# A four-layer network on one core: the hand-over from the Mamba layer to the expert layer is reordered, and each token tile gets a place of its own

## The chip, the cores and the metric

The kernel runs on one core of one Trainium2 chip. The metric is the device time of one execution in microseconds, and the lower the better. Three timed runs of the kernel before gave 2579.55, 2576.08 and 2584.2 us, so the median is 2579.55 us.

## What is computed

The input is x, 4 sequences of 512 tokens with 512 channels. Four sublayers are added to it one after the other, and the input of each sublayer is a gate: a two-sided decayed scan over the tokens of exp(k) and exp(k)*v, their quotient times sigmoid(x). In shorthand of the reference:

```python
x = x + mamba2(wkv(r=x, k=v=fside, w, u, cond), ...)        # layer 0
x = x + moe_ffn(wkv(r=x, k=v=fside, w2, u2, cond), ...)     # layer 0: 8 experts, top 2 of 8
x = x + attention(wkv(r=x, ...), ...)                       # layer 1: 16 heads, causal
x = x + ffn(wkv(r=x, ...), ...)                             # layer 1

num = nf + nb - ekv + euk * v ; den = df + db - ek + euk    # forward and backward scans
out = sigmoid(r) * (num / maximum(den, 1e-8)) * (0.8 + 0.2 * tf)

logits = tok @ gate_w.T + gate_b ; top_vals, top_idx = top_k(logits, 2)
routing = softmax(top_vals)                                 # each token goes to two experts
```

The factor num/den does not depend on x. It is computed ahead of time, on other engines, beside the layers, and is kept in DRAM ("gates"). Only sigmoid(x) has to wait for x.

## The kernel before, in words

Data lies by channel: XT holds x as 4 chunks of 128 channels (KC = 4) by 2048 tokens. There are five instruction streams, and each runs in the order in which it is written; semaphores tie them together.

**Mamba layer.** A loop runs over the four sequences b. In each, TensorE (PE) projects, ScalarE (ACT) does the activations, VectorE (DVE) the convolution taps, masks and sums. Near its end PE runs the output products (L2335) into four banks, one per channel chunk m. ACT takes the square root of the mean square (L959), DVE inverts it (`rms_inv`, L1690), and for m = 0 to 3 scales a bank (L1704) and adds it to XT (L1706, semaphore `x_added`). Between these pieces the gates of later layers are worked through in pairs of 2 tiles: ACT takes exponentials (L435, L436), DVE clamps, scans (L450, L463), takes denominators (`dens`, L478) and one reciprocal for the pair (`inverse`, L485), POOL multiplies and adds (L494 to L520), and SP stores the pair and loads the next one. The last pair of this layer is `G_MOE - 1`, in slot 0 of the gate buffers (`g_v[:, 0:2]`).

**Hand-over to the expert layer.** In the last pass of the loop (b = 3) the expert layer's inputs of sequences 0 to 2, which are finished, are made: ACT takes tanh of XT (L871, into the single buffer `tx_moe`, a part of `xdt`) and DVE multiplies it with the fetched gate in `uf1` (`moe_input`, L1506). Before the change these three stand between the four scale-and-add steps of the last sequence, so that each tanh waits for the product ahead of it to free the buffer. Sequence 3 follows in four parts (L970, L1728) as its chunks of XT are added.

PE then goes through 16 token tiles of 128 tokens (NT = 16). For tile a it transposes four 128 x 128 blocks into one of three banks (L2339), runs two filler products (`keep_busy`, L348, into a spare bank), and four logit products of 8 columns (L2359). From a = 3 on it first waits until the copy of tile a - 3 has left its bank. Ahead of tile 3 there are 12 more fillers, ahead of tile 7 there are 16. ACT (L534, even tiles) and DVE (L532, odd tiles) copy each bank into `ut`, which has 4 places, so a copy of tile a + 4 waits until SP has stored tile a in DRAM (`u_tok`, L632). SP reaches these stores only after it has stored the last gate pair.

**Routing and the first block.** With all logits there, DVE computes the top two, the places of all tokens and the gather lists in some 60 small steps (L1736 to L1831). POOL then gathers blocks of 128 tokens (L763 to L765; an indirect DMA from `u_tok`). PE transposes a block (`inputs_T`), ACT and DVE split it in two parts (L994, L1857), and PE multiplies with the split weights of an expert (L2390 to L2392). The weights are split on ACT (`split_hi`, L1025) and DVE (`split_lo`, L1842) in three pieces per expert. After the first block comes a loop over the other blocks. ACT takes the exponentials of the next gate pair (`gate(moe_pair(0), ...)`) ahead of its first block's work; the second half of these waits until POOL has finished the first result of the pair before it (`P_READY[0]`).

Of the kernel before, what the change touches and what calls it, by code (L numbers as in the profile page):

```python
# [19 lines left out]
P = 128  # L20
BATCH, T, C = 4, 512, 512
KC = C // P
# [69 lines left out]
def network(nc, xT, fT, condT, cols_d, rows_d, w_in_d, w_out_d, moe_d, gw_d, bias_d, rc_d, att_d, ffn_d, outT):  # L92
# [6 lines left out]
    with ctx:  # L99
# [74 lines left out]
        tx_moe = xdt[:, 0:2, :].rearrange("p a (h t) -> p (a h) t", h=2)  # L174
        with ExitStack() as s:
# [10 lines left out]
            bias_u = sb("bias_u", [P, 3, 2 * I_MOE], F32, s)  # L186
            idx = sb("idx", [P, NBLK], I32, s)
# [3 lines left out]
        bias_dn = g_v[:, 0:2, :]  # L191
        with ExitStack() as s:
# [13 lines left out]
            with ExitStack() as s2:  # L206
                ut = sb("ut", [P, 4, C], F32, s2)
# [75 lines left out]
        ut_stored = [sem(f"ut_stored{i}") for i in range(4)]  # L283
# [45 lines left out]
        IN_PARTS = 3  # L329
        S_, TT_, PP = bank[0:3], bank[3:5], bank[5:8]  # L330
# [192 lines left out]
        def token_copies(eng, b):  # L523

            odd = eng is nc.vector
            for tb in range(1 if odd else 0, TB, 2):
                a = b * TB + tb
                eng.wait_ge(ut_T, a + 1)
                if b:
                    eng.wait_ge(ut_stored[tb], 16 * b)  # L530
                if odd:
                    nc.vector.tensor_copy(ut[:, tb, :], UT[a % 3][:]).then_inc(ut_copied[1], 1)  # L532
                else:
                    nc.scalar.activation(ut[:, tb, :], UT[a % 3][:], ACT.Copy).then_inc(ut_copied[0], 1)  # L534
# [21 lines left out]
        def _(sp):  # L556
# [13 lines left out]
            def gates(b, last):  # L570
# [62 lines left out]
            sp.wait_ge(g_out[0], FIRST_DMA + 16 * ((G_MOE + 1) // 2))  # L633
# [53 lines left out]
        def _(pool):  # L687
# [67 lines left out]
            pair_gate(G_MOE - 1, (G_MOE - 1) % 2)  # L755
# [13 lines left out]
            for i in range(4):  # L769
                pool.wait_ge(ut_stored[i], 16 * (NT // 4))  # L770
            for j in range(3):
                gather(j, j)
            with pool.Fori(0, NBLK // MOE_BLOCKS) as trip:
# [62 lines left out]
        def _(act):  # L836
# [46 lines left out]
            with act.Fori(0, BATCH) as b:  # L883
# [73 lines left out]
                square(PAIRS - 1)  # L957
                act.wait_ge(ssq_done, PAIRS * (b + 1))
# [1770 lines left out]
```

## Time and profile before

| what | us |
|---|---|
| median of three runs | 2579.55 |
| the profiled execution, device time | 2580.49 |
| span of its trace | 2578.8 |
| PE busy | 2272.5 (88%) |
| VectorE busy | 1859.4 (72%) |
| ScalarE busy | 1002.0 (39%) |
| GpSimd (POOL) busy | 676.6 (26%) |

In all rows times are microseconds from the start of the span. DVE is VectorE, ACT is ScalarE, POOL is GpSimd and SP issues DMAs. "PEclk" is the TensorE clock that was granted: 1.00 is 2.4 GHz and 0.50 is 1.2 GHz. A timeline row gives start, duration of the whole merged piece, engine, line, what it writes and reads, how many instructions it merges, and in square brackets how long the engine stood idle before it and what ended that.

### The profile page before, as it was taken

What the parts mean: (1) busy time and instruction counts of PE and PEld (TensorE: products, weight loads), DVE (VectorE), ACT (ScalarE), POOL (GpSimd) and SP (SyncE); (2) the same over time, 40 slices, a digit from 0 to 9 for tenths busy, and PEclk for the clock granted to TensorE, in tenths of its full rate; (3) what the DMA queues carried; (4) which work ended last, traced back from release to release, by engine and by line L of the source; (5) the groups of instructions that cost most, each with busy time, mean ns of one, the idle gap of its engine ahead of it and who ended that gap; (6) DMA issues with size and microseconds to landing.
All of it is one profiled execution on the core that took longest, in us unless ns stands there. A gap on an engine that the chain in (4) does not pass through costs nothing.

```text
span 2578.8 us, 34195 instructions
## 1 busy us (share of the span) xinstructions
PE 2272.5 (88%) x10449; PEld 1672.1 (65%) x10450; DVE 1859.4 (72%) x2835; ACT 1002.0 (39%) x2073; POOL 676.6 (26%) x544
## 2 busy tenths in 40 slices
PE   0789989899898889778877999999999997999998
PEld 0344444444445677666666888888887876788886
DVE  8989898888996655556645668777777775666665
ACT  2243352352442443444434344434444443322222
POOL 5434434344342433324341011212212210000000
PEclk9999999999998899989988999999999998999999
DMA  5000001010024432343151000010000201000001
GB/s 206 17 33 33 33 16 49 17 49 18 31 82 174 154 119 66 127 164 127 60 198 46 1 33 16 17 37 21 17 29 13 65 17 49 25 25 24 24 12 65
DMA packets 52807, 148.66 MB, mean 58 GB/s; under 512 B 5008, under 2 KB 5008, under 8 KB 48336
## 3 DMA queue, kind: packets, MB, share of 16 engines
q1 hardware_dynamic: 34144, 96.08, 10.5%
q10 hardware_dynamic: 12864, 32.81, 3.5%
q0 software_dynamic: 5680, 18.62, 2.4%
q14 instruction: 97, 0.79, 0.1%
q8 instruction: 22, 0.36, 0.1%
HBM read 113.14 MB, written 34.34 MB: 57 GB/s over the span
## 4 chain that ended last, share of the span: by engine, by line
PE 37%; issue 31%; POOL 11%; DVE 8%; POOLq 6%; ACT 3%; DMA 1%; ACTq 1%; DVEq 0%; SPq 0%; another core or an unknown queue 0%
PE bank L340 9%; PE bank L341 9%; PE bank L342 9%; PE bank L2339 3%; POOLq L495 2%; POOL g_v L503 2%; POOL g_v L496 2%; PE bank L2390 2%; PE bank L2391 2%; PE bank L2392 2%; POOLq L521 1%; PE bank L2454 1%; POOLq L518 1%; POOLq L507 1%; POOL g_s L517 1%
## 5 line engine op out<-in xcount | busy, mean ns | idle before, releaser
L2214 PE MATMUL bank<-um,w_in 128*128 128x512 f32 x576 | 262.4, 609 | 3.3 <-DVE lm L1562 3.1
L2214 PEld LDWEIGHTS bank<-um,w_in 128*128 128x128 f32 x576 | 109.5, 195 | 134.8 <-issue 127.8
L340 PE MATMUL bank<-u_hi,aw_hi 128*128 (+1 forms) x384 | 158.9, 414 | 13.0 <-DVE u_lo L1955 9.1
L1182 ACT ACTIVATE probs<-bank,nmx 128x128 f32<-128x128 f32 (+3 forms) x256 | 131.5, 527 | 92.7 <-DVE nmx L1978 92.7
L1189 ACT ACTIVATE pt_hi<-bank 128x512 fp32r<-128x512 f32 (+1 forms) x192 | 94.1, 526 | 166.8 <-PE bank L2339 166.0
L341 PE MATMUL bank<-u_lo,aw_hi 128*128 (+1 forms) x384 | 152.0, 396 | 0.0
L342 PE MATMUL bank<-u_hi,aw_lo 128*128 (+1 forms) x384 | 151.9, 396 | 0.0
L1993 DVE TENSOR_TENSOR pt_lo<-bank,pt_hi 128x512 fp32r<-128x512 f32 (+1 forms) x192 | 108.8, 593 | 44.1 <-ACT pt_hi L1189 40.2
L340 PE MATMUL bank<-u_hi,fw_hi 128*128 128x512 f32 x352 | 136.9, 389 | 0.0
L341 PE MATMUL bank<-u_lo,fw_hi 128*128 128x512 f32 x352 | 136.9, 389 | 0.0
L342 PE MATMUL bank<-u_hi,fw_lo 128*128 128x512 f32 x352 | 136.9, 389 | 0.0
L2390 PE MATMUL bank<-mw,bu_hi 128*128 (+1 forms) x312 | 127.4, 408 | 10.6 <-DVE mw L1842 6.1
L450 DVE TENSOR_TENSOR_SCAN g_s<-decay,g_s 128x512 f32<-128x512 f32 x96 | 128.7, 1382 | 10.5 <-POOL g_v L496 10.5
L502 POOL TENSOR_TENSOR g_eu<-g_eu,g_s 128x512 f32<-128x512 f32 x48 | 65.6, 1366 | 253.8 <-DVE g_s L463 253.8
L1975 DVE TENSOR_REDUCE rinv<-bank 128x1 f32<-128x128 f32 (+3 forms) x256 | 107.7, 483 | 32.5 <-PE bank L2496 32.3
L2339 PE MATMUL bank<-ident,probs 128*128 128x128 f32 x640 | 94.3, 279 | 40.9 <-DVE pt_lo L1993 18.6
L463 DVE TENSOR_TENSOR_SCAN g_s<-decay,g_s 128x512 f32<-128x512 f32 x96 | 112.3, 1211 | 19.4 <-issue 18.4
L2391 PE MATMUL bank<-mw,bu_hi 128*128 (+1 forms) x312 | 123.5, 396 | 0.0
L2392 PE MATMUL bank<-mw,bu_lo 128*128 (+1 forms) x312 | 123.4, 396 | 0.0
L2162 DVE SCALAR_TENSOR_TENSOR XT<-bank,cols,XT 128x512 f32<-128x512 f32 x176 | 119.9, 742 | 3.4 <-PE bank L342 3.4
L2335 PE MATMUL bank<-xa,w_out 128*128 128x512 f32 x256 | 111.8, 592 | 0.0
L1288 ACT ACTIVATE f_t<-bank,f_sc 128x512 f32<-128x512 f32 x44 | 30.2, 687 | 209.5 <-PE bank L342 208.8
(385 smaller groups left out, 6235.3 us busy)
## 6 DMA issues: line engine op xcount, KB each, us to landing
m_stage<-in_moe SPq DMA_DIRECT2D x21, 1024.0 KB, 7.1
y_slot<-m_o ACTq DMA_DIRECT2D x39, 256.0 KB, 2.6
g_v<-in_fT SPq DMA_DIRECT2D x18, 512.0 KB, 3.3
gates<-g_v SPq DMA_DIRECT2D x18, 512.0 KB, 2.8
f_stage<-in_ffn SPq DMA_DIRECT2D x11, 768.0 KB, 4.3
u_g<-gates SPq DMA_DIRECT2D x8, 1024.0 KB, 10.1
aw_in<-in_att SPq DMA_DIRECT2D x4, 1280.0 KB
w_in<-in_w_in ACTq DMA_DIRECT2D x1, 4640.0 KB, 16.8
```

The lines of the kernel that those rows point to most:

```text
L340: nc.tensor.matmul(out, hi_w, hi_x, start=start, stop=False)
L341: nc.tensor.matmul(out, hi_w, lo_x, start=False, stop=False)
L342: return nc.tensor.matmul(out, lo_w, hi_x, start=False, stop=stop)
L450: nc.vector.tensor_tensor_scan(x, d, x, 0.0, ALU.mult, ALU.add).then_inc(g_vec, 1)
L463: nc.vector.tensor_tensor_scan(x[:, ::-1], d, x[:, ::-1], 0.0, ALU.mult, ALU.add).then_inc(g_vec, 1)
L1182: A(probs[:, h % 2, PR_AT[qb]:PR_AT[qb] + w], S_[bk][:, c0:c0 + w], ACT.Exp, bias=nmx[:, h % 2, qb:qb + 1], scale=SCALE, accum_out=rsum[:, ...
L2162: V.scalar_tensor_tensor(xm, FD[m][:], col("down_s", m), xm, ALU.mult, ALU.add).then_inc(fx_acc, 1)
L2214: mm = M(dst[:], w_in[:, k, c0:c0 + P], um[:, k, :], start=(k == 0), stop=(k == KC - 1))
L2339: return nc.tensor.transpose(out, src, ident[0:dim, 0:dim])
L2390: M(out, x_hi[:, kc, :], hi, start=False, stop=False, skip_group_check=True)
L2391: M(out, x_hi[:, kc, :], lo, start=False, stop=False, skip_group_check=True)
L2392: mm = M(out, x_lo[:, kc, :], hi, start=False, stop=(kc == KC - 1), skip_group_check=True)
```

## The change

- Expert inputs of sequences 0 to 2 (tanh on ACT, product on DVE) stand ahead of the square root and the reciprocal of the last sequence's norm. Each has its own tanh buffer (`um` and two parts of `xdt`).
- The last gate pair's scans, `dens` and `inverse` leave the loop for b = 3. The scans come after the inputs of sequence 3 on DVE, `dens` ahead of the last token copy, `inverse` after the routing tables, ahead of the first weight split. On POOL its `gate_result` comes after the first three gathers. SP stores it after the weight loads of expert 1.
- `ut` has 16 places. ACT copies tiles 0 to 11 and DVE tiles 12 to 15. No copy waits for a store.
- The down bias has its own buffer. SP issues the first up bias after all token stores have landed.
- Fillers ahead of tile 3 go from 12 to 6, ahead of tile 7 from 16 to none. The two per tile are kept.
- On ACT the exponentials of `moe_pair(0)` go from ahead of the first block's work to just ahead of the loop. On DVE `u_lo_split(0)` comes ahead of the second piece of the weight split.

```diff
-        tx_moe = xdt[:, 0:2, :].rearrange("p a (h t) -> p (a h) t", h=2)
+        tx_moe = [um[:], *(xdt[:, i:i + 2, :].rearrange("p a (h t) -> p (a h) t", h=2) for i in (0, 2))]
+            bias_dn = sb("bias_dn", [P, 2, C], F32, s)
-        bias_dn = g_v[:, 0:2, :]
-                ut = sb("ut", [P, 4, C], F32, s2)
+                ut = sb("ut", [P, NT, C], F32, s2)
+        ACT_TILES = 3 * TB
+        LAST_PAIR = G_MOE - 1, (G_MOE - 1) % 2
...
+        def token_copy(eng, a):
+            eng.wait_ge(ut_T, a + 1)
+            if eng is nc.vector:
+                nc.vector.tensor_copy(ut[:, a, :], UT[a % 3][:]).then_inc(ut_copied[1], 1)
+            else:
+                nc.scalar.activation(ut[:, a, :], UT[a % 3][:], ACT.Copy).then_inc(ut_copied[0], 1)
...  SP
-                    g_store(sp, G_MOE - 1, 0)
+            for a in range(NT):
+                sp.wait_ge(*copies(a))
+                sp.dma_start(u_dram[a * P:(a + 1) * P, :], ut[:, a, :]).then_inc(ut_stored, 16)
+            sp.wait_ge(ut_stored, 16 * NT)
             up_bias(0)
-            for a in range(NT):
-                sp.wait_ge(ut_copied[a % 2], a // 2 + 1)
-                sp.dma_start(u_dram[a * P:(a + 1) * P, :], ut[:, a % 4, :]).then_inc(ut_stored[a % 4], 16)
             for e in range(1, E):
                 stage(e)
+                if e == 1:
+                    g_store(sp, *LAST_PAIR)
...  POOL
-            pair_gate(G_MOE - 1, (G_MOE - 1) % 2)
+            for t in range(2):
+                gate_products(pool, *LAST_PAIR, t)
+            for t in range(2):
+                gate_add(pool, *LAST_PAIR, t)
+            gate_den_product(pool, *LAST_PAIR)
...
             for j in range(3):
                 gather(j, j)
+            gate_result(pool, *LAST_PAIR)
...  ACT
                 square(PAIRS - 1)
+                with act.If(b == BATCH - 1):
+                    act.wait_ge(x_added, KC * (BATCH - 1))
+                    for nxt in range(BATCH - 1):
+                        tanh_x(BATCH + nxt, nxt, tx_moe[nxt], None)
                 act.wait_ge(ssq_done, PAIRS * (b + 1))
...
-            for m in range(KC - 1):
+            for m in range(KC):
                 last_sequence(m)
-            token_copies(act, 0)
-            last_sequence(KC - 1)
             for p in range(M_PIECES):
                 o = slice(p * M_PIECE, (p + 1) * M_PIECE)
                 act.dma_start(m_stage[:, o], moe_d[0][:, o]).then_inc(m_staged[p], 16)
-            for b in range(1, BATCH):
-                token_copies(act, b)
+            for a in range(ACT_TILES):
+                token_copy(act, a)
...
-            gate(moe_pair(0), 0)
-            gate(moe_pair(0), 1)
             u_hi_copy(0)
             up_tanh(0, 0)
             fill_up(packed_of(1, True), 1)
             u_hi_copy(1)
+            gate(moe_pair(0), 0)
+            gate(moe_pair(0), 1)
...  DVE
-                scans(fourth, 0)
-                scans(fourth, 1)
+                with dve.If(b < BATCH - 1):
+                    scans(fourth, 0)
+                    scans(fourth, 1)
+                with dve.If(b == BATCH - 1):
+                    for m in range(BATCH - 1):
+                        moe_input(m)
...
+            scans(LAST_PAIR, 0)
+            scans(LAST_PAIR, 1)
+            for a in range(ACT_TILES, NT):
+                if a == NT - 1:
+                    dens(LAST_PAIR)
+                token_copy(dve, a)
...
             dve.wait_ge(route_vec, TAB_READY)
+            inverse(LAST_PAIR)
...
             split_lo(0, 0, (0,))
+            u_lo_split(0)
             split_lo(0, 0, (1,))
-            u_lo_split(0)
             split_lo(0, 0, (2,))
...  PE
-                        keep_busy({3: 12, 7: 16}.get(a, 0))
-                        pe.wait_ge(ut_copied[(a - 3) % 2], (a - 3) // 2 + 1)
+                        keep_busy({3: 6}.get(a, 0))
+                        pe.wait_ge(*copies(a - 3))
```

## Rows read from the trace of the kernel before

**Rows 1.** The page's first line, the span of the profiled execution.

```profile
span 2578.8 us, 34195 instructions
```

**Rows 2.** Busy time by stretch: stretch, length, PE, PEld, DVE, ACT, POOL, PEclk, DMA share, GB/s.

```profile
764.50:768.00 3.50, 3.50 (x11) 1.18 (x9) 2.81 (x3) 2.70 (x2) 0.00 (x0) 0.52 0.00 0
...
774.80:785.00 10.20, 9.42 (x40) 8.17 (x40) 5.78 (x7) 0.63 (x1) 4.49 (x3) 0.50 0.88 324
...
788.40:805.80 17.40, 17.40 (x137) 14.98 (x136) 4.15 (x6) 3.58 (x6) 0.00 (x0) 1.00 0.56 215
```

**Rows 3.** Timeline of PE, from the last output products to token tile 15.

```profile
744.54 15.61 PE L2335 MATMUL bank<-xa,w_out 128*128 128x512 f32 x36
...
764.37 4.44 PE L348 MATMUL bank<-causal_b,ident_b 128*128 128x512 bf16 x12
...
775.58 1.09 PE L2339 MATMUL bank<-ident,uf 128*128 128x128 f32 x4 [1.58 <-DVE ut L532]
...
785.50 5.01 PE L348 MATMUL bank<-causal_b,ident_b 128*128 128x512 bf16 x16
...
792.02 0.63 PE L2339 MATMUL bank<-ident,uf 128*128 128x128 f32 x4
...
804.01 0.64 PE L2339 MATMUL bank<-ident,uf 128*128 128x128 f32 x4
```

**Rows 4.** Timeline of DVE, from the last pair's scans to the first routing step.

```profile
739.77 4.32 DVE L450 TENSOR_TENSOR_SCAN g_s<-decay,g_s 128x512 f32<-128x512 f32 x2 [1.24 <-POOL g_v L496]
...
753.47 3.33 DVE L1690 RECIPROCAL e<-e 128x512 f32<-128x512 f32 x1
...
757.41 2.29 DVE L1506 SCALAR_TENSOR_TENSOR uf<-xdt,uf 128x2048 f32<-128x2048 f32 x1
...
764.72 0.69 DVE L1706 TENSOR_TENSOR XT<-XT,lm 128x512 f32 x1
...
773.63 1.21 DVE L1706 TENSOR_TENSOR XT<-XT,lm 128x512 f32 x1
...
805.91 0.29 DVE L1736 TENSOR_TENSOR rt<-bank,rows 128x128 f32<-128x128 f32 x1 [0.53 <-PE bank L2359]
```

**Rows 5.** Timeline of ACT, its weight loads for expert 0 and its third token copy.

```profile
774.87 1.32 ACTq L979 DMA_DIRECT2D m_stage<-in_moe  x3
789.35 0.60 ACT L534 ACTIVATE ut<-bank 128x512 f32<-128x512 f32 x1 [13.85 <-DMA u_tok<-ut]
```

**Rows 6.** Timeline of SP, the token stores.

```profile
780.87 24.86 SPq L632 DMA_DIRECT2D u_tok<-ut x16
```

**Rows 7.** The tile uf: the four fetches of gates, shortest, median and longest, and their landing.

```profile
L598 SPq DMA_DIRECT2D uf<-gates x4: 405/452/670, 739.9 to 741.9; - x4
...
DMA to landing us min/median/max: 8.9/11.1/12.8
```

**Rows 8.** Timelines at the first expert block: PE.

```profile
834.58 0.50 PE L2390 MATMUL bank<-mw,bu_hi 128*128 128x512 f32 x1 [2.08 <-DVE bu_lo L1857]
...
857.11 0.66 PE L2339 MATMUL bank<-ident,m_y 128*128 128x128 f32 x4 [1.15 <-DVE bu_lo L1857]
```

**Rows 9.** Timeline of DVE, the first two pieces of the weight split.

```profile
829.43 4.49 DVE L1842 TENSOR_TENSOR mw<-m_stage,mw 128x2048 fp32r<-128x2048 f32 x2
```

**Rows 10.** Timeline of ACT, an exponential of the gate pair and the first split of expert 1.

```profile
829.05 0.61 ACT L435 ACTIVATE g_s<-g_v 128x512 f32<-128x512 f32 x1
...
846.01 1.91 ACT L1025 ACTIVATE mw<-m_stage 128x2048 f32 x1 [3.36 <-issue]
```

**Rows 11.** Timeline of POOL, a product of the last pair's result and gathers 1 to 3.

```profile
774.25 1.72 POOL L517 TENSOR_TENSOR g_s<-g_s 128x512 f32<-128x512 f32 x1
...
832.60 2.17 POOL L765 DMA_INDIRECT ug<-u_tok,idx_now  x1 [0.84 <-issue]
...
842.03 0.97 POOL L765 DMA_INDIRECT ug<-u_tok,idx_now  x1 [5.26 <-PE bank L2339]
...
846.36 0.97 POOL L765 DMA_INDIRECT ug<-u_tok,idx_now  x1 [3.16 <-issue]
```

More of the change, by code:

```diff
@@ L282, in network @@
         ut_copied = [sem(f"ut_copied{i}") for i in range(2)]
-        ut_stored = [sem(f"ut_stored{i}") for i in range(4)]
+        ut_stored = sem("ut_stored")
         route_mm, route_vec = sem("route_mm"), sem("route_vec")
@@ L521, in gate_result, with copies @@
             eng.drain()
[L523 to L534, printed above, removed]
+        def token_copy(eng, a):
[4 more added lines that the diff above has]
+                nc.scalar.activation(ut[:, a, :], UT[a % 3][:], ACT.Copy).then_inc(ut_copied[0], 1)
+        def copies(a):
+            return (ut_copied[0], a + 1) if a < ACT_TILES else (ut_copied[1], a + 1 - ACT_TILES)
         def mamba_pair(b, r):
@@ L768, in _ @@
             pool.wait_ge(route_vec, IDX_READY)
-            for i in range(4):
-                pool.wait_ge(ut_stored[i], 16 * (NT // 4))
+            pool.wait_ge(ut_stored, 16 * NT)
             for j in range(3):
                 gather(j, j)
+            gate_result(pool, *LAST_PAIR)
             with pool.Fori(0, NBLK // MOE_BLOCKS) as trip:
@@ L961, in _ @@
                     tanh_x(b + 1, (b + 1) % BATCH, txm, b + 1)
[L962 to L965 removed]
             def last_sequence(m):
                 act.wait_ge(x_added, KC * (BATCH - 1) + m + 1)
[L970 removed]
+                A(tx_moe[1][:, m, :], XT[:, m, tok(BATCH - 1)], ACT.Tanh, scale=0.5).then_inc(last_tanh, 1)
             act.wait_ge(u_ready, FIRST + 2 * BATCH - 1)
[L973 removed]
+            for m in range(KC):
                 last_sequence(m)
[L975 to L976 removed]
             for p in range(M_PIECES):
@@ L1513, in moe_input @@
             def moe_input(b):
[L1514 removed]
+                gated(BATCH + b, uf1[:, b].rearrange("p k t -> p (k t)"), tx_moe[b].rearrange("p k t -> p (k t)"), g_fetched[b], 1)
             mamba_input(0)
@@ L1692, in _ @@
                     mamba_input(b + 1)
-                dens(fourth)
+                    dens(fourth)
                 for m in range(KC):
-                    if m < BATCH - 1:
-                        with dve.If(b == BATCH - 1):
-                            moe_input(m)
-                    else:
-                        inverse(fourth)
+                    if m == KC - 1:
+                        with dve.If(b < BATCH - 1):
+                            inverse(fourth)
                     if m == 0:
@@ L1796, in _ @@
             dve.wait_ge(route_mm, U_DONE)
-            for i in range(4):
-                dve.wait_ge(ut_stored[i], 16 * (NT // 4))
+            dve.wait_ge(ut_stored, 16 * NT)
             route.inc(V.tensor_tensor(oh_r[:], choices(2, P), rconst("iota", P).unsqueeze(1).to_broadcast([P, 2 * NT, P]),
@@ L2367, in _ @@
             M(LGP[:, 256:384], ones[:], gt2, start=True, stop=True).then_inc(route_mm, 1)
-            for i in range(2):
-                pe.wait_ge(ut_copied[i], NT // 2)
+            pe.wait_ge(ut_copied[0], ACT_TILES)
+            pe.wait_ge(ut_copied[1], NT - ACT_TILES)
             pe.wait_ge(dve_step, DVE_MAMBA * BATCH + AT_PREFIX)
```

15 lines of the change are left out of this document (2 added, 13 removed).

## The prediction

> **What bounds the kernel now.** The span is 2578.8 us [rows 1]. I read the PE timeline of the stretch that the change touches first, then the other engines' timelines for what each PE gap waits for, and last the granted clock by stretch. The loop passes before the last one and everything after the first expert blocks run the same instructions in the same order, so only about 740 to 860 us can change, and what PE does there sets the start of all that follows.
>
> In this stretch PE finishes the output products at 744.54 + 15.61 = 760.15 [rows 3]. Three token tiles later it runs 12 fillers (764.37) and then loses time in three ways. The copies come late: tile 4 starts at 775.58 after an idle wait for DVE [rows 3], because DVE makes its last addition to XT only at 773.63 [rows 4]. The copies of tiles 4 to 7 then wait for a store: ACT stood idle for 13.85 us until the store of tile 0 had landed, and its copy starts at 789.35 [rows 5]; SP had issued that store at 780.87, behind the last gate pair [rows 6]. And the clock is at 0.50 from 774.8 to 785.0 [rows 2], so that tiles 4 to 6 take (785.50 - 775.58) / 3 = 3.31 us each, whereas tiles 8 to 15 take (804.01 - 792.02) / 7 = 1.71 us each at 1.00 [rows 2, 3]. From tile 8 on PE is never idle and bounds the chain. The first routing step of DVE at 805.91 [rows 4] follows the last logit product at once, and it heads a serial chain of small steps to the first weight split at 829.43 [rows 9]. So: whatever moves the end of tile 15 moves the rest one for one.
>
> **The change, part by part.**
>
> *Inputs ahead of the norm, scans away.* DVE no longer runs the pair's scans from 739.77 to 753.47 (13.7 us) [rows 4]. In their place it has three products of 2.29 us. These wait for the gates, which SP issues from 739.9 to 741.9 and which land 8.9 to 12.8 us after their issue [rows 7]: the last at about 754.7, the third, with a median of 11.1 from about 741, at about 752. So product 2 ends at 752 + 2.3 = 754.3, the reciprocal (3.33) [rows 4] at about 757.7, which is 0.9 us later than today's 753.47 + 3.33 = 756.8. The freed scans hardly help here, since the fetch is late next. The gain comes behind it: no product or tanh wait stands between the four additions. One scaling and one addition take 2 x 0.69 plus a small gap, say 1.5 us [rows 4], so the last addition ends at 757.7 + 4 x 1.5 = 763.7, against 773.63 + 1.21 = 774.84. The output products end at 760.15, in time for it. The three tanh on ACT fall into the time in which it waits for PE's sum of squares; they cost nothing unless they last beyond 752.
>
> *Token copies.* After the last addition ACT does one tanh (0.6), issues the three weight loads (1.32, which overlaps the tanh as it does at 774.87) [rows 5] and copies tile 0 (0.60): it is out at about 763.8 + 1.3 + 0.6 = 765.7, and tile 3 can start at 765.8. PE by then has its three tiles and 6 fillers behind it: 12 fillers took 4.44, partly at the low clock [rows 3], so 6 end between 765.3 and 766.5. From there no copy waits for a store, and ACT needs 0.6 us per tile against PE's 1.71, so PE runs through. Tile 15 starts at 765.8 + 12 x 1.71 = 786.4 instead of 804.01: **17.6 us earlier, if the clock is at 1.00**. The last store is issued a microsecond after that tile and has the whole routing chain (23.5 us from 805.91 to 829.43) [rows 4, 9] to land in; so has the first up bias, which now queues on SP behind the stores, and the down bias. Without this cover each would cost its landing, some 2 to 8 us.
>
> *Scans, dens, store of the last pair.* DVE has the scans (13.7) from about 766 to 780, and its first token copy is tile 12, transposed at 765.8 + 9 x 1.71 = 781.2. They fit by a hair; an overrun of 3 us would delay tile 15's bank by less than that. POOL's additions lie beside them. The store on SP goes behind expert 1's loads; the loads of expert 2 behind it wait for splits that come later anyway. I take 0 for these, between 0 and 2.
>
> *Inverse ahead of the first split.* On DVE 3.33 us are put ahead of the split at 829.43 (times from here on in the old count, so with the gain of 17.6 taken off later). One piece is 4.49 / 2 = 2.24 [rows 9]. The input's low part then follows after one piece instead of two: today it takes 834.58 - (829.43 + 4.49) = 0.66 after the second piece until PE starts, and from now on 829.43 + 3.33 + 2.24 + 0.66 = 835.7; PE's first expert product moves from 834.58 [rows 8] to 835.7, **+1.1 us**, not +3.3. Today POOL is done with the second block's gather only at 842 [rows 11], after PE's first 24 expert products, so little of it reaches the second block: I take 0.2.
>
> *Exponentials ahead of the loop.* ACT's four exponentials (0.61 each) [rows 10] lay in idle time ahead of the first block. Now they lie between the copy that ends at 846.01 - 3.36 = 842.65 and the loop's entry, which takes 3.36 us of issue before the first split at 846.01 [rows 10]. From this split hang DVE's split and its low part, on which PE waits at 857.11 [rows 8], without slack. The least cost is 4 x 0.61 + 0.2 = 2.6 us. But the second half also waits until POOL has done the third of four products of `gate_result`, which is now behind gather 2, with a drain between. Gather 1 starts at 832.60 as before. A gather that meets no weight loads takes 846.36 - 842.03 = 4.3 us, gather 1, which met them, kept POOL for 842.03 - 832.60 = 9.4 us [rows 11]. In the new order the loads start some 3 us later (the split that frees their buffer is later), so gather 1 is fast and gather 2 starts at 836.9, into the loads: POOL's drain ends at about 836.9 + 8.7 = 845.6, the third product (1.3 to 1.72) [rows 11] at 846.9. Exponentials until 848.1, loop entry 3.36: the split starts at 851.5, **+5.5 us**. If gather 1 meets the loads as well, gather 2 starts at 842.03 and ends at 851 and the cost is 10.6. So the bounds are 2.6 and 10.6, and I take 5.5, since it is built on the measured gathers. The 1.1 of the paragraph above is inside it.
>
> **The sum.** The profiled execution took 2580.49 us (span 2578.8 and 1.7 around it), 0.9 more than the median 2579.55. 2580.5 - 17.6 + 5.5 = 2568.4, and I say 2568. The clock's ups and downs in the first expert blocks shift by a few us with it; that is in the range.
>
> **The clock, the open question.** In the profile the clock fell at 764.5, with PE busy all through (3.50 of 3.50 in that stretch) [rows 2], after the three token tiles that have no fillers; it rose after the 12 fillers, and it rose again only within the 16 fillers of 785.50. From 774.8 to 785.0 PE ran token tiles with two fillers each and stayed at 0.50; from 788.4 to 805.8 it ran the same tiles and stayed at 1.00 [rows 2, 3]. So this work keeps either level that it finds, and the change takes out most of the fillers that lifted it. What decides is whether the clock falls in tiles 0 to 2, which end at 764. The new order starts these 0.3 us earlier and puts fillers right behind them as before; the trace holds one execution, in which it fell, and nothing in it says that it must fall in each. I give it 3 in 10.
> The Trainium skill, in "TensorE: Matmul & The Clock Gate", section "What's actually happening", says that the slow level is the default and that activity releases it, and its section on oscillation lays the fall to idle gaps of PE. By this rule tiles without idle time would neither lose the clock nor stay slow, and the result would be the forecast alone; the rows above show a fall and a long stay without idle time, so here the trace decides against it, and the low case stands.
>
> **The rivals.**
>
> *A. The clock falls in tiles 0 to 2 and nothing lifts it (slower).* Then tiles 3 to 15 take 3.31 us each. Tile 15 starts at 766 + 12 x 3.31 = 805.7, 1.7 later than today, and takes 1.6 longer itself: +3.3. With the 5.5 of the hand-over: 2580.5 + 3.3 + 5.5 = 2589.3. It decides from the point at which more than about 7 of the 13 tiles run at 0.50 (7 x 1.6 = 11.2 of the net 12.1 us eaten). For it: the fall at 764.5 and the 10 us at 0.50 [rows 2]. Against it: the same tiles held 1.00 for 17 us [rows 2].
>
> *B. The hand-over stalls more.* ACT's exponentials wait behind POOL's gathers at the upper bound: 2580.5 - 17.6 + 10.6 = 2573.5, and with a fall of the clock in the longer PE gap up to 2576. For it: gather 1's 9.4 us [rows 11]. Against it: the later loads.
>
> *C. The hand-over costs only the exponentials.* 2580.5 - 17.6 + 2.6 = 2565.5, a little less if some are hidden. For it: gathers of 4.3 us.
>
> *D. The change does not do what it says,* since the fetched gates (to 754.7) hold the norm up. At 3 us later for each addition this would give 2571; it is part of the range.
>
> **How the numbers follow.** Forecast with its variants (D) 0.55, at 2568 (own range 2564 to 2573); A 0.25 (0.3 of the executions, and the median needs most of them), B 0.12, C 0.08. For a range with 8 in 10 I must take in most of A: low 2562, high 2590. About 0.3% is what a measurement of this kernel can tell from no change, that is below 2571.8 or above 2587.3. Faster: 0.47 of the forecast, C, and 0.02 of B: 0.57. Same: 0.08 of the forecast, 0.10 of B, 0.07 of A: 0.25. Slower: 0.18 of A.
>
> **What would show it.** Right: the last addition to XT at about 763 to 764; no wait of a copy for a store; tile 3 to tile 15 in 20.6 us with PEclk 1.00; first routing step at about 788.3; ACT's exponentials of the pair behind its second input copy, with an idle time in the middle ended by POOL, and a PE gap of 3 to 6 us ahead of the third block's input. Wrong: PEclk 0.50 over the tiles (A); additions that still wait; a first routing step later than 792 at full clock; or no POOL wait in ACT (C). The forecast fails altogether if a stretch outside 740 to 860 moves.

## The result, and the profile after

The changed kernel took 2561.56 us (median; 2557.01 to 2565.08), beside 2579.55 (2576.08 to 2586.71) for the kernel before in the same comparison. The ratio is 0.9926, with a 95% interval of 0.9914 to 0.9937: faster by 0.74%, or 18 us. The forecast was 2568 with a range from 2562 to 2590, so the sign was right and the median lies 0.4 us below the range. Its profiled execution was the longest, 2565.08 us (span 2563.4). Of all executions of this study two lie far outside, 7877.76 us of r4_inverse_exps_early and 3646.75 us of the kernel before in the second comparison; they are left out of the medians and ratios below.

Granted clock and busy time by stretch of the kernel after (columns as in rows 2):

```profile
760.00:764.50 4.50, 4.50 (x40) 4.10 (x39) 4.07 (x7) 3.07 (x4) 0.00 (x0) 1.00 0.01 4
764.50:768.00 3.50, 1.94 (x13) 1.09 (x11) 3.50 (x6) 2.33 (x5) 0.00 (x0) 1.00 0.52 162
768.00:789.20 21.20, 21.20 (x177) 19.34 (x176) 14.32 (x16) 5.15 (x9) 7.88 (x5) 1.00 0.84 321
```

Timeline of PE, token tiles 0 to 15 and the first expert blocks, of the kernel after:

```profile
760.12 0.60 PE L2347 MATMUL bank<-ident,uf 128*128 128x128 f32 x4
...
763.93 1.46 PE L350 MATMUL bank<-causal_b,ident_b 128*128 128x512 bf16 x6
766.95 0.66 PE L2347 MATMUL bank<-ident,uf 128*128 128x128 f32 x4 [1.56 <-ACT ut L531]
...
787.53 0.64 PE L2347 MATMUL bank<-ident,uf 128*128 128x128 f32 x4
...
819.16 0.72 PE L2398 MATMUL bank<-mw,bu_hi 128*128 128x512 f32 x1 [3.15 <-DVE bu_lo L1865]
...
845.04 0.66 PE L2347 MATMUL bank<-ident,m_y 128*128 128x128 f32 x4 [0.62 <-DVE bu_lo L1865]
857.58 1.11 PE L2347 MATMUL bank<-ident,ug 128*128 128x128 f32 x4 [5.60 <-DVE by_lo L1887]
```

Timeline of DVE: the expert inputs, the norm, the last addition, the first routing step.

```profile
747.18 2.29 DVE L1510 SCALAR_TENSOR_TENSOR uf<-um,uf 128x2048 f32<-128x2048 f32 x1 [8.51 <-DMA uf<-gates]
...
753.30 2.29 DVE L1510 SCALAR_TENSOR_TENSOR uf<-xdt,uf 128x2048 f32<-128x2048 f32 x1 [0.80 <-DMA uf<-gates]
755.51 3.35 DVE L1698 RECIPROCAL e<-e 128x512 f32<-128x512 f32 x1
...
764.19 0.69 DVE L1712 TENSOR_TENSOR XT<-XT,lm 128x512 f32 x1
...
789.50 0.29 DVE L1744 TENSOR_TENSOR rt<-bank,rows 128x128 f32<-128x128 f32 x1 [0.60 <-PE bank L2367]
```

Timeline of ACT: the first token copies, the third exponential of the pair, the first split of expert 1.

```profile
766.30 2.06 ACT L531 ACTIVATE ut<-bank 128x512 f32<-128x512 f32 x4 [0.76 <-issue]
...
829.54 0.63 ACT L437 ACTIVATE g_s<-g_v 128x512 f32<-128x512 f32 x1 [0.82 <-POOL g_v L521]
...
834.15 1.92 ACT L1029 ACTIVATE mw<-m_stage 128x2048 f32 x1 [3.37 <-issue]
```

Timeline of POOL: the third product of the last pair's result, two gathers and a product of the next gate pair behind them.

```profile
828.17 1.27 POOL L521 TENSOR_TENSOR g_v<-g_v,g_s 128x512 f32<-128x512 f32 x1 [2.26 <-issue]
...
832.35 1.01 POOL L771 DMA_INDIRECT ug<-u_tok,idx_now  x1 [0.76 <-issue]
836.95 2.58 POOL L771 DMA_INDIRECT ug<-u_tok,idx_now  x1 [3.39 <-issue]
...
845.56 2.78 POOL L498 TENSOR_TENSOR g_v<-g_eu,g_v 128x512 f32<-128x512 f32 x1 [4.72 <-issue]
```

The three losses of [rows 2, 3] are gone. PE waits once more, 1.56 us ahead of tile 3, and then runs twelve tiles in 787.53 - 766.95 = 20.58 us, 1.715 each, with the clock at 1.00. No copy waits for a store. The first routing step comes at 789.50 instead of 805.91 [rows 4], 16.4 us earlier. At the first product of expert 0 the gain is 834.58 - 819.16 = 15.4 [rows 8], at the third block's input 857.11 - 845.04 = 12.1 [rows 8]. (These two rows transpose `m_y`, the second block's middle result, right ahead of the third block's first products; the prediction calls the place the third block's input, and so does the text below. `ug` at 857.58 is the input of the fourth block.) The span is shorter by 15.4.

### The profile page after: what moved, and what is told of

It reads as the page before. It is cut to its first block, busy times and chain, and to the rows that moved or that the text cites. A ratio compares the mean times of both kernels' runs of the same rounds, so it can differ in the third digit from the quotient of the medians.

```text
span 2563.4 us, 34103 instructions
## 1 busy us (share of the span) xinstructions
PE 2258.9 (88%) x10411; PEld 1666.8 (65%) x10428; DVE 1853.6 (72%) x2831; ACT 1003.0 (39%) x2076; POOL 675.8 (26%) x544
## 4 chain that ended last, share of the span: by engine, by line
PE 38%; issue 30%; POOL 10%; DVE 8%; POOLq 6%; ACT 4%; DMA 2%; ACTq 1%; another core or an unknown queue 0%; DVEq 0%; SPq 0%
PE bank L342 9%; PE bank L344 9%; PE bank L343 9%; PE bank L2347 3%; PE bank L2398 2%; PE bank L2400 2%; PE bank L2399 2%; POOLq L497 2%; POOL g_v L498 2%; POOL g_v L505 2%; POOLq L523 1%; POOLq L520 1%; POOL g_s L519 1%; POOLq L509 1%; POOL g_eu L504 1%
## 6 DMA issues: line engine op xcount, KB each, us to landing
u_g<-gates SPq DMA_DIRECT2D x8, 1024.0 KB, 10.7
```

## The experiments

All kernels compute all of the reference; only filler products, whose results nobody reads, are added or left out. Three theories stood against each other. T1, the forecast's: the tile stretch gives the gain, the hand-over to the expert blocks costs some 4 to 5 us of it, and this passes on to the end. T2: what is late in the expert blocks is another thing, so the hand-over's delay is taken back there. T3: the granted clock in the tile stretch decides, and the fillers that were kept decide the clock. "Before" is the kernel before in the same comparison, since the three comparisons ran on three chips and its median differs from one to the next (2578.14 in the first, 2572.07 in the second, 2579.85 in the third). The second one holds no execution of the changed kernel, so its runs are set against before or each other. The ratio with its interval is an estimate from all the executions and not the quotient of the two medians.

| run | median, us (lowest to highest) | before | ratio, 95% |
|---|---|---|---|
| r1_after_again | 2558.34 (2554.83 to 2577.55) | 2578.14 | 0.9939 (0.9919 to 0.9959) |
| r2_scans_back | 2570.28 (2567.18 to 2577.5) | 2578.14 | 0.9974 (0.9962 to 0.9985) |
| r3_inverse_early | 2560.44 (2559.17 to 2585.93) | 2578.14 | 0.9939 (0.9924 to 0.9954) |
| r4_inverse_exps_early | 2563.16 (2550.64 to 2569.05) | 2578.14 | 0.9947 (0.9927 to 0.9966) |
| r5_places_only | 2566.28 (2564.81 to 2575.37) | 2572.07 | 0.9981 (0.9971 to 0.9991) |
| r6_places_few_fillers | 2575.97 (2571.65 to 2584.36) | 2572.07 | 1.0018 (1.0008 to 1.0029) |
| r7_no_six | 2575.38 (2571.7 to 2578.52) | 2572.07 | 1.0014 (1.0005 to 1.0023) |
| r8_fillers_back | 2558.95 (2554.97 to 2562.55) | 2572.07 | 0.9947 (0.9933 to 0.9961) |
| r9_after_third | 2563.04 (2557.78 to 2584.4) | 2579.85 | 0.9945 (0.9926 to 0.9964) |
| r10_products_first | 2555.57 (2551.74 to 2572.47) | 2579.85 | 0.9917 (0.9895 to 0.9938) |
| r11_fill_first_three | 2567.1 (2560.89 to 2569.42) | 2579.85 | 0.9946 (0.9933 to 0.9959) |
| r12_all_three | 2554.26 (2551.69 to 2556.71) | 2579.85 | 0.9900 (0.9886 to 0.9914) |

### The changed kernel again

> The changed kernel once more, unchanged, on another chip, to see how far single executions lie apart and whether the tile stretch ever runs at the low clock. Theory 1 (the route start is set by the last addition and 13 tiles at 1.71 us; the rest of the spread comes from clock falls in the expert blocks): 2557 to 2566 us, tiles 3 to 15 in 20.6 us at PEclk 1.00, and no execution near 2580. Rival 1 (the clock falls in tiles 0 to 2 in some executions): one or two executions of five lie 18 to 22 us above the others, at 2578 to 2585.

> The changed kernel a third time, unchanged, as the yardstick for the three kernels of this call, since the kernel before gave 2578.1 us as the median of one call and 2572.1 of the other. Theory 1: 2554 to 2566 us, and, as the highest of nine executions in the first call (2577.55) hints, perhaps one execution some 18 us above the others with the tiles at the low clock.

No edit in either. The medians are 19.8 and 16.8 us below those of before; with the 18.0 of the first comparison the gain is 17 to 20 us. Of the 26 executions of this kernel three stand apart, 2577.55, 2582.99 and 2584.4, with a mean granted clock of 0.951 to 0.952 over the whole execution where the others had 0.958 or more. None of the three was traced. Rival A had them at 3 in 10. Two other kernels with the same PE tile code have one such execution each: r3 2585.93 (0.951) and r10 2572.47 (0.954). The expectation for r1 under T1 had none near 2580 and missed; its rival had one or two in five.

### What the six fillers are for

```diff
 r7_no_six, against the changed kernel
-                        keep_busy({3: 6}.get(a, 0))
 r8_fillers_back, against the changed kernel
-                        keep_busy({3: 6}.get(a, 0))
+                        keep_busy({3: 12, 7: 16}.get(a, 0))
```

> The changed kernel without the 6 fillers ahead of tile 3. PE then waits idle for about 3 us (763.9 to 766.9) for ACT's first copy. If the clock falls there and tile work does not lift it: tiles of 3.31 us, the first routing step about 18 to 20 us later, 2580 us. If the fillers there do nothing: the same time as the changed kernel within 1 us.

> The changed kernel with 12 fillers ahead of tile 3 and 16 ahead of tile 7, as before the change. At the full clock a filler is 0.21 to 0.23 us. Ahead of tile 3 the first 12 fit nearly into the wait for ACT (763.9 to 766.95); the 16 add 3.5 us to PE. Theory 1 (PE bounds the tiles and has no idle time): 3.5 us more than the changed kernel. Rival (PE has slack there): 0 to 1 us.

Busy time and granted clock by stretch of r7_no_six (columns as in rows 2):

```profile
764.50:768.00 3.50, 0.58 (x3) 0.58 (x4) 3.36 (x7) 1.94 (x5) 0.00 (x0) 0.63 0.41 122
768.00:785.00 17.00, 17.00 (x74) 14.80 (x73) 11.22 (x10) 3.33 (x6) 6.72 (x4) 0.50 0.78 300
785.00:806.00 21.00, 21.00 (x90) 18.07 (x89) 2.44 (x5) 2.39 (x4) 0.00 (x0) 0.50 0.20 76
```

Its PE timeline, tiles 3 and 15:

```profile
767.42 1.11 PE L2347 MATMUL bank<-ident,uf 128*128 128x128 f32 x4 [3.08 <-ACT ut L531]
...
807.12 1.09 PE L2347 MATMUL bank<-ident,uf 128*128 128x128 f32 x4
```

Without the six, PE stands idle for 3.08 us ahead of tile 3, the clock falls there, and all twelve tiles take (807.12 - 767.42) / 12 = 3.31 us, though PE is busy all through: 19.1 us lost up to tile 15. All executions of r7 lie between 2571.7 and 2578.5, 16 us above r8 in the median and 3 us above before; the expectation had 2580. So six bf16 products of 1.46 us in all carry nearly the whole gain of the change, seen through before's median. With all the old fillers back (r8) the clock stays at 1.00 too and tile 15 starts at 792.11, 24.0 us after tile 3 instead of 20.6: the fillers cost 3.4 us there, once nothing stalls behind them. r8 lies 13.1 us below before, where the changed kernel lies 17 to 20 below it in the other two comparisons; that fits the 3.5 us expected, without a direct comparison.

The profiled execution of r3 (its edit is below) happened to be one of the rare long ones, 2585.93 us against 2559 to 2564 for the others of its kernel, and shows what happened in it. Busy time and granted clock by stretch of r3_inverse_early:

```profile
764.50:768.00 3.50, 2.29 (x16) 1.32 (x14) 3.36 (x6) 1.56 (x4) 0.00 (x0) 1.00 0.16 29
768.00:785.00 17.00, 16.44 (x75) 14.42 (x76) 13.23 (x14) 4.37 (x9) 8.05 (x5) 0.56 0.85 319
```

Its PE timeline, tiles 3, 4 and 15:

```profile
768.56 0.66 PE L2348 MATMUL bank<-ident,uf 128*128 128x128 f32 x4 [1.77 <-ACT ut L531]
...
770.64 1.09 PE L2348 MATMUL bank<-ident,uf 128*128 128x128 f32 x4
...
807.01 1.09 PE L2348 MATMUL bank<-ident,uf 128*128 128x128 f32 x4
```

The six fillers are there, the wait ahead of tile 3 is 1.77 us instead of 1.56, and the clock falls in tile 3; from 770.64 each tile takes 3.31 us. What follows the fall is rival A's mechanism, at its price: the two long executions of r9 lie 20.0 and 21.4 us above their median, the one of r1 19.2, and the forecast had 2589.3 - 2568.4 = 20.9. That these three fell in the same way is likely by their mean clock and their time, and not traced. The Trainium skill, in "TensorE: Matmul & The Clock Gate", section "HAM oscillation — how this bites in real kernels", lays a fall to idle gaps of PE. The falls in r7 and r3 follow one. For the fall at 764.5 in the kernel before [rows 2] the prediction says that PE had no idle time, but it had, ahead of tile 0. Timeline of PE of the kernel before, tiles 0 and 7:

```profile
760.53 0.63 PE L2339 MATMUL bank<-ident,uf 128*128 128x128 f32 x4 [0.38 <-DVE lm L1704]
...
790.35 0.60 PE L2339 MATMUL bank<-ident,uf 128*128 128x128 f32 x4
```

r5 and r6, which keep the old order, have the same wait (0.38 and 0.39 us) and the same fall behind tiles 0 to 2, with PE busy in between; in the ten traces that have no wait there, the clock holds over tiles 0 to 2. So the prediction's sentence that the trace decides against that rule is not safe. Whether so short a wait is the cause was not tested by itself.

### The places alone, and with few fillers

```diff
 both, against the kernel before
-                ut = sb("ut", [P, 4, C], F32, s2)
+                ut = sb("ut", [P, NT, C], F32, s2)
...
-                if b:
-                    eng.wait_ge(ut_stored[tb], 16 * b)
 r6_places_few_fillers besides
-                        keep_busy({3: 12, 7: 16}.get(a, 0))
+                        keep_busy({3: 6}.get(a, 0))
```

> The kernel before with one part of the change alone: ut has 16 places and no copy waits for a store (the first up bias is fetched after the stores, since its buffer lies under the larger ut). Fillers stay at 12 and 16. Theory 1 (the 16 fillers ahead of tile 7 had run in the time of the store wait, so PE itself was not idle): PE's work is the same, 0 to 1 us of change against before; the ACT wait of 13.85 us for the store vanishes without effect. Rival 4 (the store wait set the pace): 5 to 9 us less than before.

> As the kernel before with 16 places, and with 6 fillers ahead of tile 3 and none ahead of tile 7, as in the change, but with the late additions of before, so that PE waits for copies at tiles 3 and 4. Rival 1's mechanism (tile work with two fillers keeps a low clock once it is low): PEclk 0.50 from about 771 to the end of tile 15, tiles of 3.31 us, the last routing input at about 775.6 + 12 x 3.31 = 815, 9 to 11 us later than before: about 2590. Theory that the clock recovers by itself within the tile work: it rises some tiles later, and the 5.0 us of fillers are saved: 2572 to 2577.

In both, SP issues the first up bias behind the token stores. ACT's copy of tile 4, which stood for 13.85 us behind a store [rows 5], no longer does. Timeline of ACT of r5_places_only, its copies of tiles 4 and 6:

```profile
777.80 0.60 ACT L532 ACTIVATE ut<-bank 128x512 f32<-128x512 f32 x1 [1.21 <-PE bank L2339]
784.41 0.60 ACT L532 ACTIVATE ut<-bank 128x512 f32<-128x512 f32 x1 [6.02 <-PE bank L2339]
```

Its PE timeline, tile 3, the sixteen fillers and tile 15:

```profile
771.98 0.76 PE L2339 MATMUL bank<-ident,uf 128*128 128x128 f32 x4 [2.07 <-ACT ut L532]
...
786.59 5.02 PE L348 MATMUL bank<-causal_b,ident_b 128*128 128x512 bf16 x16
...
805.11 0.64 PE L2339 MATMUL bank<-ident,uf 128*128 128x128 f32 x4
```

Yet tile 3 to tile 15 takes 33.1 us as before (805.11 - 771.98; 804.01 - 770.88 there): PE had spent the store wait in its sixteen fillers, so in these two traces the largest idle time of the profile was worth nothing in the tile stretch. The medians say otherwise: 2572.07 and 2566.28 are 5.8 us apart, where T1 expected 0 to 1 and the rival, that the store wait set the pace, 5 to 9. The traced execution (2571.36) lies 5.1 us above r5's median, so it can't speak for the others. In the kernel before the copy of tile 4 ended at 789.35 + 0.60 = 789.95 and PE went on at 790.35, so the fillers covered the store wait by 0.4 us only, at the clock of that execution. In the two traces r5 is 1.1 us behind at the first routing step (807.00) and 5.7 ahead at the last expert block (1270.17 and 1275.83). What the 5.8 us are stays open.

In r6 the clock falls behind tiles 0 to 2 as in the kernel before [rows 2], six fillers with a wait of 3.89 us behind them don't lift it, tiles 3 to 15 run at 0.50, and tile 15 starts at 811.61 (expected 815). The median is 9.7 us above r5's but 3.9 above before, where 9 to 11 above before were expected: the time lies in the range of the other theory (2572 to 2577), whose mechanism, a clock that rises by itself within the tiles, the trace rules out. The few fillers pay only together with the new order.

### The last pair's scans back ahead of the inputs

```diff
-                with dve.If(b < BATCH - 1):
-                    scans(fourth, 0)
-                    scans(fourth, 1)
+                scans(fourth, 0)
+                scans(fourth, 1)
...
-            scans(LAST_PAIR, 0)
-            scans(LAST_PAIR, 1)
```

> The changed kernel with the last pair's scans back in the loop, on DVE ahead of the three expert inputs, so that these start at 753.5 as the scans did end before. Theory 1: the last addition to XT ends at 753.5 + 6.9 + 3.35 + 6.0 = 769.8 instead of 764.9, so the time is 4.9 us above that of the changed kernel. Rival 2 (moving the scans brings nothing, since the fetched gates land late and the chain waits for something else): 0 to 1 us.

Timeline of DVE of r2_scans_back:

```profile
741.11 4.34 DVE L452 TENSOR_TENSOR_SCAN g_s<-decay,g_s 128x512 f32<-128x512 f32 x2 [1.26 <-POOL g_v L498]
...
754.83 2.27 DVE L1510 SCALAR_TENSOR_TENSOR uf<-um,uf 128x2048 f32<-128x2048 f32 x1
757.01 6.62 DVE L1510 SCALAR_TENSOR_TENSOR uf<-xdt,uf 128x2048 f32<-128x2048 f32 x2
763.56 3.34 DVE L1697 RECIPROCAL e<-e 128x512 f32<-128x512 f32 x1
```

Its POOL timeline at the same time:

```profile
754.99 3.23 POOL L504 TENSOR_TENSOR g_eu<-g_eu,g_s 128x512 f32<-128x512 f32 x1 [2.48 <-DVE g_s L465]
758.18 3.31 POOL L505 TENSOR_TENSOR g_v<-g_v,g_s 128x512 f32<-128x512 f32 x1
```

The reciprocal comes at 763.56 instead of 755.51, 8.05 us later. I had expected 4.9. The scans began 1.3 us later than in the kernel before, and two of the products took 3.35 us each instead of 2.29; together 3.4, about what was missing. POOL's additions lie beside them, but the first product lies beside one as well and took 2.27, so what made the two long is not shown. Tile 0 then starts at 767.9 instead of 760.12, the tiles run at 0.50 until the clock rises at 779.4 in tile 3, behind the six fillers and with no wait between, and the median is 12 us above r1's. So moving the scans was needed: the sentence "the freed scans hardly help here" is right only against the old order, in which no product stood ahead of the norm. With the products ahead, the scans' move is worth 12 of the 20 us.

### The hand-over, undone in two steps

```diff
 r3_inverse_early, against the changed kernel
-                if a == NT - 1:
+                if a == ACT_TILES:
                     dens(LAST_PAIR)
                 token_copy(dve, a)
+                if a == ACT_TILES:
+                    inverse(LAST_PAIR)
...
-            inverse(LAST_PAIR)
...  POOL
+            gate_result(pool, *LAST_PAIR)
             for j in range(3):
                 gather(j, j)
-            gate_result(pool, *LAST_PAIR)
 r4_inverse_exps_early besides, on ACT
+            gate(moe_pair(0), 0)
+            gate(moe_pair(0), 1)
             u_hi_copy(0)
...
             u_hi_copy(1)
-            gate(moe_pair(0), 0)
-            gate(moe_pair(0), 1)
```

> The changed kernel with the last pair's dens ahead of DVE's first token copy, its inverse right behind that copy, where DVE waits for PE, and gate_result on POOL ahead of the gathers. The exponentials stay ahead of the loop. Theory 1 (the inverse in front of the first split and POOL behind the gathers cost the hand-over): the first expert product starts 1.6 us earlier against the last routing step, PE's gap there falls from 3.15 to about 1.5 us, which also spares the low clock behind it, and the first split of expert 1 starts 3.8 us earlier: 3 to 4 us less time. Rival 3 (the expert blocks take up a late start, since PE waits there anyway): 0 to 1 us.

> As the kernel with the early inverse, and ACT's exponentials of the next pair back ahead of the first block's work, where ACT is idle. Theory 1: another 2.5 us (four exponentials of 0.61) in front of the split of expert 1, so 5.5 to 6.5 us less than the changed kernel: about 2555. Rival 3: no difference to the kernel with the early inverse beyond 1 us.

Neither gains, where 3 to 4 and 5.5 to 6.5 us were expected: 2560.44 and 2563.16, beside 2558.34 for r1. Timeline of PE of r4_inverse_exps_early, at the third block and behind it:

```profile
839.46 0.66 PE L2348 MATMUL bank<-ident,m_y 128*128 128x128 f32 x4 [0.42 <-DVE bu_lo L1866]
856.65 1.11 PE L2348 MATMUL bank<-ident,ug 128*128 128x128 f32 x4 [10.20 <-DVE by_lo L1888]
```

Its DVE timeline, the next pair's scans:

```profile
847.64 4.28 DVE L452 TENSOR_TENSOR_SCAN g_s<-decay,g_s 128x512 f32<-128x512 f32 x2 [5.91 <-POOL g_v L498]
```

Its POOL timeline, a gather and the product that the scans wait for:

```profile
831.95 0.97 POOL L772 DMA_INDIRECT ug<-u_tok,idx_now  x1 [7.40 <-issue]
...
846.22 1.26 POOL L498 TENSOR_TENSOR g_v<-g_eu,g_v 128x512 f32<-128x512 f32 x1 [6.65 <-issue]
```

The two steps do what T1 says up to the third block: its input is transposed at 839.46 instead of 845.04, 5.6 us earlier (0.5 of it is there at the first routing step already, 788.96 and 789.50). Then PE stands for 10.20 us instead of 5.60, and the next block's `ug` comes at 856.65 instead of 857.58: 4.7 of the 5.6 are given back. What is late there is POOL's product (L498) of the next gate pair. It stands on POOL behind two gathers and a drain (an instruction of the kernel between L496 and L498), comes at 846.22 against 845.56 in the changed kernel, however early ACT was, and DVE stands idle ahead of its scans until then, with the `by_lo` that PE waits for behind them. This is T2, up to this block.

### POOL's products ahead of the gathers

```diff
+                gate_products(pool, k, s, 0)
+                gate_products(pool, k, s, 1)
                 ahead(0)
                 ahead(1)
-                gate_products(pool, k, s, 0)
-                gate_products(pool, k, s, 1)
                 ahead(2)
```

> The changed kernel with one swap on POOL: in each pass of the expert loop the two gate products stand ahead of the two gathers. Theory 2 (what is late after the hand-over is POOL: the product on which DVE's forward scan waits is queued behind gathers 3 and 4, which are slow beside the weight loads, and DVE's low part of the block, on which PE waits 5.6 us, is queued behind that scan): the PE gap ahead of the fourth block's input falls from 5.6 to about 3 us, 2 to 3 us less time. Rival 5 (the gap is set by the scans themselves): no change within 1 us.

If the product's place behind the gathers is what is late, this must gain where r3 and r4 didn't. Timeline of POOL of r10_products_first, its last product of the pair:

```profile
835.92 1.29 POOL L498 TENSOR_TENSOR g_v<-g_eu,g_v 128x512 f32<-128x512 f32 x1
```

Its PE timeline, at the third block, behind it and at the last block:

```profile
844.89 0.60 PE L2347 MATMUL bank<-ident,m_y 128*128 128x128 f32 x4
853.34 0.86 PE L2347 MATMUL bank<-ident,ug 128*128 128x128 f32 x4 [2.22 <-DVE by_lo L1887]
...
1250.54 0.60 PE L2347 MATMUL bank<-ident,m_y 128*128 128x128 f32 x4
```

The products end at 837.2, PE's wait falls from 5.60 to 2.22 us, and its `ug` comes 4.2 us earlier with the same start at the third block. The median is 2555.57, 7.5 us below the changed kernel's 2563.04 in the same comparison, though the two intervals overlap by 0.1%. That is more than the 2 to 3 us expected: the swap acts in every pass of the expert loop, and the last expert block comes at 1250.54, against 1255.46 to 1260.85 in the three traces of the changed kernel. T2 is confirmed for this wait.

### Fillers in tiles 0 to 2, and all together

```diff
 r11_fill_first_three, against the changed kernel (r12_all_three has r4's and r10's edits as well)
-                    if a >= 3:
-                        keep_busy(2)
+                    keep_busy(2)
```

> The changed kernel with two fillers in tiles 0 to 2 as well. These lie in the time in which PE waits for ACT's first copy anyway (idle 1.56 us). Rival 1's mechanism (the clock falls, in some executions, over the tiles without fillers, and stays low to the end of tile 15): the same median within 2 us, but no execution 15 to 25 us above the others. If the slow executions come from elsewhere, they stay.

> The early inverse, the early exponentials, the gate products ahead of the gathers and the fillers in tiles 0 to 2 together. Theory 2: the early hand-over gained 5.6 us up to the second block and lost 4.7 of it in a PE gap of 10.2 us, in which DVE waited for POOL's product. With the products first the gap is 3 to 5 us and the gain stays: 5 to 8 us less than the changed kernel, about 2551 to 2555. Rival 3 (the expert blocks take up a late start by themselves): no gain beyond that of the kernel with the products first.

PE timeline of r12_all_three, at the same places:

```profile
840.76 0.66 PE L2348 MATMUL bank<-ident,m_y 128*128 128x128 f32 x4 [1.19 <-DVE bu_lo L1866]
849.89 0.65 PE L2348 MATMUL bank<-ident,ug 128*128 128x128 f32 x4 [0.69 <-DVE by_lo L1888]
...
1249.14 0.60 PE L2348 MATMUL bank<-ident,m_y 128*128 128x128 f32 x4
```

r11 starts tile 15 at 786.9, like the changed kernel, and shows no execution at the low clock, but with 3 in 26 for the changed kernel five executions can't show that it prevents them; its median is 4 us higher. In r12 PE waits 0.69 us ahead of `ug`, which comes 7.7 us earlier than in the changed kernel, so the early hand-over gets past the wait that took it back in r4. But it does not last to the end. Set against r10, which has POOL's products first and the late hand-over, r12 is 4.1 us ahead at the third block (844.89 - 840.76), and 1.4 at the last (1250.54 - 1249.14), about what it had at the first routing step (788.52 against 789.82). The medians are 1.3 us apart, with intervals that overlap, so the rival of r12's expectation, no gain beyond r10's, is not refuted: the expert blocks took the early start back a second time, and by what is open. At 2554.26 us, ratio 0.9900, it is the fastest kernel of the study, 25.6 us below before and 8.8 below the changed kernel.

## Why the prediction was right or wrong

**Inputs ahead of the norm: right, within 1.3 us.** The last product ended at 753.30 + 2.29 = 755.6 (forecast 754.3), each held up by its fetch as said (SP issued the fetches from 740.93 instead of 739.90), and the last addition at 764.19 + 0.69 = 764.9 (763.7, from 774.84).

**Copies and tiles: right.** Tile 3 at 766.95 (765.8), then 20.58 us to tile 15 (20.6). The first routing step came 16.4 us earlier instead of 17.6, which is the 1.2 us of the late fetch. Scans, `dens`, stores and the bias loads cost nothing that shows. D, additions that wait for the fetch by 3 us each time, did not come.

**Hand-over up to the third block: right to 0.3 us in place, 1.2 us too dear.** The first expert product lost 16.4 - 15.4 = 1.0 us (1.1). The third of POOL's products ended at 829.44 (846.9 - 17.6 = 829.3), the exponentials followed it, and the first split came at 834.15 (851.5 - 17.6 = 833.9). At the third block the gain was 12.1, as the sum had it; but from a first routing step that was 16.4 earlier, not 17.6, so the hand-over cost 4.3 us up to there instead of 5.5, and the two errors cancel. B and C fall: gathers 1 and 2 did not both meet the loads, and there was a wait for POOL.

**From there to the end: the step that failed.** "Whatever moves the end of tile 15 moves the rest one for one", and with it the 5.5 us of the hand-over, put into the sum whole. r4 shows that undoing it brings 5.6 us at the third block, 0.9 one block later and 1.1 at the last expert block; r12 against r10 shows 4.1 at the third block and 1.4 at the last. So a late or early hand-over is for the most part taken up within the expert blocks, at first by the wait for POOL's product; what takes up the rest is open. With 16.4 and some 1 us instead of 17.6 and 5.5, the sum is 2580.5 - 16.4 + 1 = 2565.1, and the profiled execution took 2565.08. That fit is better than its proof, and partly luck: in the pair of profiles themselves the gain is 12.1 at the third block, falls to 10.7 and grows to 15.0 only by the last one. What made it grow is not shown. Timeline of PE of the kernel before, the last expert block:

```profile
1275.83 0.60 PE L2339 MATMUL bank<-ident,m_y 128*128 128x128 f32 x4
```

The same of the kernel after:

```profile
1260.85 0.60 PE L2347 MATMUL bank<-ident,m_y 128*128 128x128 f32 x4
```

Besides, between the third block and a later one the profiled executions of the changed kernel differ among themselves by up to 4.6 us.

**The width: the range lacked a term.** It was built from mechanisms, for one execution, and set against a median. The three profiled executions of the changed kernel reach the last expert block at 1260.85, 1260.16 and 1255.46, and the attention stage alone, from its first projection to the first product of the ffn, lasted 886.5 to 897.0 us in the traces of this study, in unchanged code. Before's profiled execution was 0.9 above its median, after's 3.5 above. A low end some 5 us lower would have held all three medians (2561.56, 2558.34, 2563.04). Of the 17 to 20 us gained in the medians, 15 to 16 have their place in the traces (16.4 less the hand-over); the rest stays open, since the kernel before was traced in one execution. The places alone (r5) are 5.8 us below before in the median, with no place in a trace either, so the new order need not be the source of the whole gain; no run has the new order without the new places.

**A: right in price, wrong in where the clock falls and how often.** 19 to 21 us above the median (forecast 20.9), in 3 of 26 executions rather than 3 in 10. In r7 it is the rule. That the clock falls in the wait ahead of tile 3 or just behind it, not in tiles 0 to 2, was not foreseen: in r3 and r7 it follows PE's wait there, of which the six fillers cover half.

## What to carry to other kernels

Price a delay at the next places where engines meet, not at its own: 5.6 us won at one block were 0.9 one block later, because a queue there (POOL's product behind two gathers) was late anyway. Look for that queue first: putting the product ahead was worth 7.5 us, while the early hand-over added no more than 1.3 to it. The longest idle time of a profile (13.85 us behind a store) can be hidden behind another engine's work in the execution that was traced, and its removal can still move the median, so test it by itself and trace more than one execution. Six filler products of 1.46 us together were worth 19 us, so take filler work out one group at a time with a wait beside it in view. A forecast for a median needs the spread between executions as a term of its own.

## What the runs showed of the hardware

- **The clock and the same work.** Token tiles with two fillers each held 1.00 for 20.6 us (after) and 0.50 for 40 us (r7), PE busy throughout in both. Over these stretches they kept the level that they found. It rose in r2's tile 3, right behind six fillers, and within the sixteen of the kernel before. Ahead of tile 3 a wait of 1.77 us was followed by a fall (r3); waits of 1.28 to 1.65 us were not (r4, r9, r1, after, r10). These are single executions, and no limit follows from them.
- **Gathers beside weight loads.** From issue to landing the gathers of the changed kernel took 3.3 to 8.4 us, and up to 9.9 in r10. POOL's product L498, which stands behind a drain, waits when gathers stand ahead of it (4.72 us in after, 6.65 in r4) and does not when they stand behind (0.15 in r10). The Trainium skill, in "DMA: Bandwidth & Descriptors", section "Issuing engines are not separate DMA queues", says that transfers of all issuing engines interleave on the same 16 DMA engines; the slow landings beside loads that SP issued agree.
- **DVE beside POOL.** The product of 128x2048 took 2.29 us with POOL idle (after). In r2 the first of three took 2.27 beside a POOL addition, which itself took 3.23 instead of 1.26; the second, beside the next addition, took 3.35; the third took 3.35 with POOL busy in its first third only. The Trainium skill, in "GPSIMD Engine Reference", section "Specifications", has the two engines share their SBUF interfaces, with contention for DVE instructions of two SBUF inputs. The first two rows agree with it, with the price paid now by one engine and now by the other; the third is not explained by it.
